# An eight-layer network in one kernel: steps of the selective scan moved one later

## The reference, cut to what matters

```
xn      = layernorm(x) * ln_w + ln_b
x_in, z = split(xn @ W_in)
xc      = silu(conv(x_in, 4 taps, causal) + conv_b)
dt_r, Bm, Cm = split(xc @ W_xproj)            # 8, 16, 16 columns
dt      = softplus(dt_r @ W_dt + b_dt)
h[t]    = h[t-1] * exp(dt[t] * A) + dt[t] * Bm[t] * xc[t]   # per channel and state
y[t]    = sum over the states of h[t] * Cm[t]
y       = (y + xc * D) * silu(z)
out     = x + y @ W_out
```

## Time and profile before

| | us |
|---|---|
| median of 3 runs | 2778.79 |
| lowest and highest | 2772.78 and 2779.42 |
| the profiled execution's own time | 2771.78 |
| its span, first to last instruction | 2770.0 |
| the 128 scans, first start to last end | 900.4 to 1327.0 |

### The profile page before, as it was taken

How to read it: one execution, slowest core, us unless ns; L and a number is a source line. 1 busy time by engine, 2 the same in 40 slices (tenths; PEclk the granted TensorE clock), 3 DMA queues, 4 the chain that set the end, 5 groups by cost and what they waited for, 6 DMA issues and landing times. The chain is left out here.

```text
span 2770.0 us, 42642 instructions
## 1 busy us (share of the span) xinstructions
PE 2480.3 (90%) x13253; PEld 1589.3 (57%) x13280; DVE 1740.7 (63%) x4100; ACT 1433.8 (52%) x2908; POOL 1615.9 (58%) x1421
## 2 busy tenths in 40 slices
PE   7977787799578899997579899999999999999999
PEld 4756777687565344433379734444444445777776
DVE  4436444575424999999756599999999992211112
ACT  3431333334246877775334377777777774333333
POOL 4742555442364999999145376777767771997000
PEclk9988999899788999999889999999999999999999
DMA  9011333500012232322520068888888884000001
GB/s 295 25 35 49 109 107 108 165 1 24 26 40 73 93 98 91 96 97 88 175 80 25 14 142 196 192 191 191 191 195 187 194 193 100 9 16 9 8 8 31
DMA packets 148262, 274.82 MB, mean 99 GB/s; under 512 B 29003, under 2 KB 68694, under 8 KB 148038
## 3 DMA queue, kind: packets, MB, share of 16 engines
q1 hardware_dynamic: 135798, 251.75, 35.2%
q0 software_dynamic: 9088, 18.63, 2.4%
q10 hardware_dynamic: 3152, 1.71, 0.3%
HBM read 102.97 MB, written 24.58 MB: 46 GB/s over the span
## 5 line engine op out<-in xcount | busy, mean ns | idle before, releaser
L1784 POOL TENSOR_TENSOR l3a_p_all<-l3a_p_all,l3a_rden 128x1024 f32<-128x1024 f32 x256 | 483.7, 1893 | 202.2 <-DVE l3a_rden L1859 202.1
L1917 ACT ACTIVATE l3a_p_all<-l3a_p_all,l3a_low 128x512 f32<-128x512 f32 x512 | 364.3, 713 | 129.8 <-DVE l3a_low L1854 128.5
L1854 DVE CUSTOM_DVE_ANT_0 l3a_p_all<-bank,relative_bias 128x512 f32<-128x512 f32 x512 | 331.9, 686 | 53.9 <-PE bank L1983 30.5
L1867 DVE STREAM_TRANSPOSE l3a_blocks<-l3a_p_all 128x1024 f32<-128x1024 f32 x256 | 313.9, 1235 | 1.8 <-issue 1.8
L2784 POOL TENSOR_TENSOR l2a_dBu<-l2a_du,l2a_bs 128x1024 f32<-128x1024 f32 x128 | 298.5, 2352 | 17.4 <-DVE l2a_h L3020 16.2
L3020 DVE TENSOR_TENSOR_SCAN l2a_h<-bank,l2a_dBu 128x1024 f32<-128x1024 f32 x128 | 290.9, 2281 | 11.9 <-POOL l2a_dBu L2784 6.5
L1841 DVE SCALAR_TENSOR_TENSOR x<-bank,l3a_blocks,x 128x128 f32<-128x128 f32 x256 | 71.9, 344 | 336.5 <-PE bank L2058 336.3
L1932 ACT ACTIVATE relative_bias<-bank,l3a_b 128x512 f32<-128x512 f32 x224 | 153.3, 687 | 214.1 <-PE bank L2048 210.8
L1983 PE MATMUL bank<-l3a_kT,l3a_qT 64*128 64x512 f32 x1024 | 245.3, 607 | 3.1 <-DVE l3a_low L1854 2.6
L2009 PE MATMUL bank<-l3a_pT,l3a_v 128*64 128x512 f32 x1024 | 233.8, 598 | 0.1
L2048 PE MATMUL bank<-relative_xnT_all,relative_w_qk 128*128 128x512 f32 x512 | 231.0, 595 | 0.0
(11 more groups left out here) (532 smaller groups left out, 4964.3 us busy)
## 6 DMA issues: line engine op xcount, KB each, us to landing
l3a_pT<-l3a_blocks SPq DMA_DIRECT2D x1024, 128.0 KB
l2a_bs<-l2a_b_rows SPq DMA_DIRECT2D x128, 256.0 KB, 3.1
l0fe_wv<-expert_weights SPq DMA_DIRECT2D x71, 256.0 KB
by_place<-by_distance SPq DMA_DIRECT2D x16, 512.0 KB, 12.6
relative_bias<-by_place SPq DMA_DIRECT2D x16, 448.0 KB, 11.3
l2a_c_rows<-l2a_b_rows SPq DMA_DIRECT2D x24, 256.0 KB
expert_weights<-in_L_ffn_in_dram SPq DMA_DIRECT2D x1, 4096.0 KB, 29.1
l0f_answers<-l0f_y_rows SPq DMA_DIRECT2D x16, 256.0 KB, 5.2
```

The costliest lines, as they stand in the source:

```text
L1784: p_ready.by(pool.tensor_tensor(a, a, bcast(rden[g % 2][:, t, :], n_after=S), ALU.mult))
L1854: bk.drain(dve.tensor_tensor_reduce(p_of(g, t)[:, h, :], ps(job)[:], bias[:, u * 2 + h, b0:b0 + S], 1.0, 3.0e38, ALU.add, ALU.min, low[:, ...
L1867: ins = dve.transpose(out, p_of(g, t).rearrange("p h (k b j) -> p (h k) b j", b=Q, j=32))
L1917: ins = act.activation(a, a, ACT.Exp, bias=low[:, t, h:h + 1], scale=-1.0, accum_out=den[:, t, h:h + 1])
```

## The change

In sequences 1 to 7 these move one step later: on TensorE the four pieces of the convolution and the two products of z; on ScalarE the two copies out of the convolution, the two copies of z, and both silus; on VectorE `add`. In sequence 0 the expressions with `late // 2` had the later step already, and there nothing changes; `add` does not run in it. The projection, `keep_normed`, `take_bc`, `give_out`, the list `order` and GpSimd's and SyncE's loops are as before. In the convolution's order the new expression `(0, 1) if n % 2 else (2, 3)` takes the first two taps at steps 7 and 9.

```diff
@@ -2976,11 +2976,11 @@
                             rows_of(q + 2)
                         if n == 5 + late:
                             affine(q + 2)
-                        if n in (9 + late // 2, 11 + late // 2):
-                            take_conv(q + 2, (n - 9) // 2)
-                    if n in (12 + late // 2, 13 + late // 2):
-                        take_z(q, n - 12 - late // 2)
-                    if n == 13 + late // 2:
+                        if n in (10, 12):
+                            take_conv(q + 2, (n - 10) // 2)
+                    if n in (13, 14):
+                        take_z(q, n - 13)
+                    if n == 14:
                         if q + 2 < B:
                             silu_xc(q + 2)
                         silu_z(q)
@@ -3070,7 +3070,7 @@
                         weigh(m)
                     if n == 1 and q:
                         finish(q - 1)
-                    if n == 6 and q:
+                    if n == 7 and q:
                         add(q - 1)
                 finish(B - 1)
                 add(B - 1)
@@ -3198,14 +3198,13 @@
                         step_sizes(q + 1, 0)
                     if n == 4 and q:
                         give_out(q - 1)
-                    if n in (10 + late // 2, 11 + late // 2):
-                        gate(q, n - 10 - late // 2)
+                    if n in (11, 12):
+                        gate(q, n - 11)
                     if q + 2 < B:
                         if n == 3 + late:
                             turn(q + 2)
-                        first = 6 + late // 2
-                        if n in range(first, first + 4):
-                            conv(q + 2, (n - first) // 2, (2, 3) if (n - first) % 2 else (0, 1))
+                        if n in range(7, 11):
+                            conv(q + 2, (n - 7) // 2, (0, 1) if n % 2 else (2, 3))
                         if n == 14:
                             project(q + 2)
                 give_out(B - 1)
```

## The result

Over 17 runs each the changed kernel took 2787.53 us (median) and the kernel before 2778.55; the ratio is 1.0032, with a 95% interval of 1.0024 to 1.0041. So it is 9 us slower, against 4.1 forecast: a small loss, just past the 0.3% under which the prediction would not have told it from none.

What follows compares the result with a forecast made beforehand. VectorE was read as busiest, but TensorE, running without a pause mid-sequence, as setting what follows. The terms 4.5 - 0.2 - 0.2 = +4.1 us on the median 2778.79 gave 2782.9 us, range 2771 to 2791.

Steps and rivals of the forecast that it cites:

- TensorE's queue sets the middle of a sequence: TensorE, busy 29.39 of 29.50 us in sequence 2 up to the projection, delivers late what VectorE waits for.
- The add gives nothing: Before `add` on VectorE: the 1.19 us wait goes, 0.9 returns as a wait for C; taken as 0 in sequences 2 to 4.
- The second z product 3.65 us later: On TensorE, the second z product comes after three more items and ends at 1060.68, not 1057.03.
- 9.35 us from its end to state 2: Distance from the second z product's end to the next sequence's state 2 scan, read in sequence 0.
- 0.90 us a sequence: The state 2 scan behind each of sequences 1 to 5 starts 0.90 us later, +4.5 us in all.
- Sequence 6 gains 0.2: With no convolution left and one silu less, sequence 6 loses its one 0.23 us wait: -0.2 us.
- Sequence 7, -0.2 forecast: Where TensorE has room, moving `add` gains up to 0.25 us in sequence 7, taken at -0.2.
- The clock: About 1 us stands before TensorE's fillers, spread to five sequences, were taken to bring no falls: nothing added.
- The rival by which the falls move away: The three falls beside the turn don't come back, returning 3.5 us: +0.6 us, 2779.4; chance 0.17.
- The sum: Whole kernel: 4.5 - 0.2 - 0.2 = +4.1 us, laid on the median 2778.79.
- slower by over 0.3%: Whole kernel slower by over 8.3 us; chance 0.13, of it 0.10 from the clock and 0.03 from the forecast's tail.
- the rival in which the fillers bring falls: The 1 us stand before TensorE's fillers brings a 3.4 us half-speed fall in five sequences: +12.6, 2791.4; chance 0.12.

Runs made afterwards that it cites:

- the null edit: The kernel before with one small activation (128x1) added behind ScalarE's loop of the scan; ratio to before 0.9990, scan stage 427.4 us.
- z ahead: The changed kernel with TensorE's product of z put ahead of the adding-up of GpSimd's part in the same step; ratio to before 1.0000, scan stage 421.2 us.
- `keep_normed` at 12: The changed kernel with `keep_normed` at step 12 and not 15; ratio to before 1.0017, scan stage 429.7 us.
- z and silus only: The kernel before with only z's two products, their copies and both silus one step later; ratio to before 1.0030, scan stage 430.7 us.
- The second comparison: The changed kernel run again without an edit, on another chip, against the kernel before; ratio 1.0019, scan stage 429.8 us.

## Why the prediction was right, and where it was not

- **TensorE's queue sets the middle of a sequence.** Right, and the heart of it. In sequence 2 of the changed kernel it is busy for 33.13 of 33.35 us from 1037.40 to 1070.75, and one product put ahead of one adding-up in it gives back 1.7 us a sequence.
- **The add gives nothing.** Right: with only `add` moved the wait turned into one of 0.95 us for C (0.9 forecast) where the clock falls. What I did not say is that the move needs the convolution's move, or it costs 0.6 a sequence.
- **The second z product 3.65 us later; 9.35 us from its end to state 2.** The three items take 3.65 in the changed kernel too: 1064.22 - 1060.57. But the product itself comes later by more. In sequence 1, at full clock in both kernels, first before and then changed:

```profile
1001.96 1.02 PE L3101 MATMUL bank<-l2a_turned,scan_packed 128*128 128x512 f32 x2
```

```profile
966.56 2.29 DVE L3020 TENSOR_TENSOR_SCAN l2a_h<-bank,l2a_dBu 128x1024 f32<-128x1024 f32 x1 [0.47 <-ACT bank L2921]
...
1010.21 1.02 PE L3101 MATMUL bank<-l2a_turned,scan_packed 128*128 128x512 f32 x2
```

  From the scan of state 2 it is 1001.96 - 962.20 = 39.76 us before and 1010.21 - 966.56 = 43.65 changed: 3.89 later. In the sequences with a fall it is 3.6 to 3.8. The 9.35 was measured as 1074.58 - (1064.22 + 1.02) = 9.34. Sequence 0 of the kernel before was the right place to read it.
- **0.90 us a sequence.** Mis-sized at full clock: 54.01 - 52.87 = 1.14, and the term that was too small is the 3.65. I worked it out on sequence 2, in which the clock's fall held TensorE behind VectorE; there it fits (54.9 to 55.05 against 54.05). At full clock TensorE comes up to VectorE at step 9. TensorE's spread of step 9 and VectorE's weighing that it waits for:

```profile
1046.83 0.38 PE L3124 MATMUL bank<-l2a_bc,scan_pick 128*128 128x512 bf16 x1
```

```profile
1045.50 1.19 DVE L3029 TENSOR_TENSOR l2a_hc<-l2a_h,bank 128x1024 f32<-128x1024 f32 x1
```

  The weighing ends at 1045.50 + 1.19 = 1046.69 and the spread starts 0.14 later. With the convolution a step later TensorE has nothing else to run there; before, one more piece of the convolution (1.7 us) stood in front of that spread. The spread comes 0.23 us later than it would without the stand, which is what 3.65 lacks to 3.89.
- **Sequence 6 gains 0.2.** Wrong in sign. State 1 of sequence 7 waits 0.57 for its decay behind the lone silu of z, and the sequence takes 52.08 against 51.72: +0.4. I had said that one silu less is enough. Sequence 7, -0.2 forecast: from its state 2 to the end it takes 46.2 and 44.9 in the two profiles of the changed kernel against 45.2 before, but the null edit, which moves nothing, also takes 44.9. What differs is where a fall meets it. With only `add` moved and the fall at the same step as before it takes 44.95, which is the gain that was forecast.
- **The clock.** No new fall came of the 1.01 us stand before the fillers: that rival did not come true. By the rule of the Trainium skill ("TensorE: Matmul & The Clock Gate", section "A second HAM failure mode: psum-queue depth-cycling"), by which short idle spells, often enough, bring falls, the five new stands should have brought some; none of the falls in sequences 1 to 6 lies beside one. The falls that there were lie beside the 1.45 us wait before the turn, as before:

```profile
1088.61 1.09 PE L3085 MATMUL bank<-ident,l2a_rows 128*128 128x128 f32 x4 [1.45 <-ACT l2a_dt L2899]
...
1089.92 2.77 PE L3141 MATMUL bank<-l2a_hc,ident 128*128 128x512 f32 x4
```

```profile
1096.45 1.22 DVE L3029 TENSOR_TENSOR l2a_hc<-l2a_h,bank 128x1024 f32<-128x1024 f32 x1 [0.69 <-remote]
1097.59 0.68 DVE L3041 TENSOR_TENSOR x<-bank,x 128x512 f32<-128x512 f32 x1
```

  The adding-up took 2.77 us (1.88 at full clock), and VectorE waited 0.69 for C at step 7, though `add` behind it no longer waits. Where the wait before the turn stands whole, a run has 1 to 4 such falls in sequences 1 to 5, at about 1 us each, and their number differs between runs of one kernel. It is the largest noise in the stage. The rival by which the falls move away had something to it: the changed kernel had two and one where the kernel before had three and three. But with z ahead, `keep_normed` at 12 and z and silus only it was two, four and one, so that no run shows that the move was the cause.
- **The sum.** +4.1 forecast; +5.5 and +3.2 on the stage in two profiles, and 0.9 each behind the last scan, a term that the sum put at nothing. That sequences 1 to 5 came out at +4.1 and +3.1 us, near the +4.5 forecast, is in part luck: at equal falls they would have lost 1.14 or 0.9 each, about 5.0, and one and two falls fewer gave some of it back. The second comparison gives +0.19%, 5.3 us, the first 9.0 between the medians. What lies above the layer's 4 to 6 us in the first is not pinned to any stage: outside the scans the same program differed by several us between two profiles. The 9.0 us lie above the band of +2 to +6, which had a chance of 0.47, and in the case "slower by over 0.3%", which had 0.13. The stated range covers them only because it was drawn up to the rival in which the fillers bring falls, and that rival did not come true. The second comparison's 5.3 lies in the band.

What stays open: why z ahead, whose stage is 5.4 us shorter, measured a ratio of no less than 0.999. It is the largest of a row. All nine comparisons of a kernel with a step moved came out 0.8 to 4.5 us above what its stage and the tail behind it explain; the unchanged kernel came out 1.4 above, the null edit 3.6 below. Each has 2.5 to 5 us of noise, and those run together share their times of the kernel before, so chance can do it. No run rules out a small cost outside the stage either.

## What to carry to other kernels

When steps of several engines are moved together, follow the last product that the moved step waits for, and count what now stands in front of it in its own engine's queue, and where that engine now catches up with the one that feeds it; the step's number in the consumer's loop is the smaller part. A wait that goes away before a full queue comes back at the next thing which that queue delivers. Look in the profile for a place where the new order already runs (here the first sequence): a distance read there held to 0.01 us. And check an edit by the length of the stage it touches, since some us of a 2.8 ms kernel drown in the rest.

## What the runs showed of the hardware

The chips that ran these kernels fall into two groups: the kernel before took 2771 to 2779 us on some and 2692 on others, with the scan stage equal to 0.1 us (426.6 and 426.5). The difference lies in front of the scan: its first scan starts at 900.4 on the one and 828.0 on the other, while the part behind the last scan differs by 7.5 us. Most of it lies between the first and the last indirect transfer of the first expert layer: 266.6 us in the one profile, 208.8 in the other.

A wait of 1.45 us on TensorE had a fall to half clock beside it only in some sequences, 23 of 45 (nine runs, sequences 1 to 5 of each). Once it was broken into 0.96 and 0.69 with 2.5 us of products between there was none in 15 sequences (three runs).
